# Nine of sixteen products by C on GpSimd instead of eight, in a four-layer selective scan

## The reference

```
dA = exp(d_t[:, :, None] * A)
h = dA * h + (d_t * u_t)[:, :, None] * b_t[:, None, :]
y = einsum('bdn,bn->bd', h, c_t)
```

## Time and profile before

| what | value |
|---|---|
| runs | 2176.87, 2178.3, 2180.0 us |
| median | 2178.3 us |
| the profiled execution's own time | 2175.6 us |
| its span, first to last instruction | 2173.8 us |
| mean granted TensorE clock | 0.942 |
| busy: PE, DVE, ACT, POOL | 1875.8, 1943.6, 1682.6, 1460.3 us |
| stretch of the steps in steady state | about 150 to 1640 us |
| stretch of the experts | about 1732 to 2174 us |

### The profile page before, as it was taken

How to read it: one execution, slowest core, us unless ns; L and a number is a source line. 1 busy time by engine, 2 the same in 40 slices (tenths; PEclk the granted TensorE clock), 3 DMA queues, 4 the chain that set the end, 5 groups by cost and what they waited for, 6 DMA issues and landing times.

```text
span 2173.8 us, 34586 instructions
## 1 busy us (share of the span) xinstructions
PE 1875.8 (86%) x10784; PEld 1179.1 (54%) x10784; DVE 1943.6 (89%) x1824; ACT 1682.6 (77%) x3050; POOL 1460.3 (67%) x1365
## 2 busy tenths in 40 slices
PE   4588888888888888888888888888887599999998
PEld 1344444444444444444454444444444289998998
DVE  3699999999999999999999999999999877776775
ACT  3799999998999999999999898999998233333343
POOL 1588888888888888888888888888889400000000
PEclk8799999999999999999999999999999799999999
DMA  7233232323232323233333323232324100000000
GB/s 235 79 77 84 71 77 61 77 61 77 61 77 62 81 65 80 69 79 77 79 80 80 77 61 77 61 77 61 77 62 119 35 1 11 11 11 10 10 6 11
DMA packets 73289, 139.45 MB, mean 64 GB/s; under 512 B 13072, under 2 KB 31120, under 8 KB 68624
## 3 DMA queue, kind: packets, MB, share of 16 engines
q1 hardware_dynamic: 66832, 120.32, 22.9%
q10 hardware_dynamic: 6400, 18.42, 3.7%
HBM read 63.85 MB, written 7.74 MB: 33 GB/s over the span
## 4 chain that ended last, share of the span: by engine, by line
ACT 29%; POOL 26%; PE 25%; issue 12%; DVE 5%; SPq 1%; DMA 1%; ACTq 1%; POOLq 0%; DVEq 0%
POOL scan L466 12%; ACT decay L545 11%; POOL scan L460 11%; PE y_ps L1216 11%; PE dbu_ps L1192 8%; ACT scan L623 7%; DVE scan L800 3%; POOL scan L457 2%; ACT sp_e L582 2%; ACT delta L583 2%; ACT sp_l L592 2%; PE dbu_ps L1016 2%; ACT sp_e L587 1%; SPq L351 1%; ACT du_t L608 1%
## 5 line engine op out<-in xcount | busy, mean ns | idle before, releaser
L800 DVE TENSOR_TENSOR_SCAN scan<-decay,dbu_ps 128x1024 f32<-128x1024 f32 x512 | 1154.8, 2274 | 47.2 <-PE dbu_ps L1016 40.3
L1016 PE MATMUL dbu_ps<-ident,scan 128*128 128x128 f32 x4096 | 570.4, 286 | 236.4 <-DVE scan L800 198.8
L466 POOL TENSOR_TENSOR scan<-scan,c_rep 128x1024 f32<-128x1024 f32 x256 | 676.3, 2642 | 140.8 <-DVE scan L800 75.8
L1016 PEld LDWEIGHTS dbu_ps<-ident,scan 128*128 128x128 f32 x4096 | 479.8, 146 | 516.6 <-DVE scan L800 266.6
L545 ACT ACTIVATE decay<-d_rep,a_cur 128x510 f32<-128x510 f32 x1024 | 668.1, 709 | 72.0 <-DMA d_rep<-delta 29.6
L460 POOL TENSOR_SCALAR scan<-du_t,b_t 128x256 f32<-128x256 f32 x896 | 592.7, 677 | 0.0
L623 ACT ACTIVATE scan<-du_t,b_t 128x256 f32<-128x256 f32 x1024 | 445.6, 494 | 1.2
L809 DVE TENSOR_TENSOR scan<-scan,c_rep 128x1024 f32<-128x1024 f32 x256 | 330.8, 1292 | 0.0
L738 ACT ACTIVATE decay<-dbu_ps 128x512 f32<-128x512 f32 x256 | 148.5, 598 | 207.0 <-PE dbu_ps L1192 195.6
L1001 PE MATMUL y_ps<-scan,sel 128*32 128x512 f32 x2048 | 301.8, 664 | 5.7 <-POOL scan L466 5.7
L1029 PE MATMUL pre_ps<-xn,w_pre 128*128 128x512 f32 x512 | 248.4, 608 | 5.6 <-DVE w_pre L789 4.8
(11 more groups left out here) (105 smaller groups left out, 1784.5 us busy)
## 6 DMA issues: line engine op xcount, KB each, us to landing
d_rep<-delta SPq DMA_DIRECT2D x512, 128.0 KB, 3.1
c_rep<-c_rows SPq DMA_DIRECT2D x32, 1024.0 KB
w_pre<-prepared_weights ACTq DMA_DIRECT2D x15, 866.0 KB, 13.8
prepared_weights<-scan SPq DMA_DIRECT2D x3, 1122.0 KB, 26.9
scan<-in_conv_w SPq DMA_DIRECT2D x4, 512.0 KB, 4.9
w_out<-prepared_weights SPq DMA_DIRECT2D x16, 128.0 KB, 13.3
sp_e<-in_x_rows SPq DMA_DIRECT2D x8, 256.0 KB, 3.4
d_rep<-in_w ACTq DMA_DIRECT2D x2, 1024.0 KB, 7.3
```

The source lines that it names most:

```text
L466: nc.gpsimd.tensor_tensor(ring[slot % RING], ring[slot % RING], c_rep[par][:, slot // PRS, :].unsqueeze(1).broadcast_to([128, 2, TG]), ALU ...
L800: nc.vector.tensor_tensor_scan(ring[slot % RING].rearrange("p u t -> p (u t)"), decay[slot % DEC].rearrange("p u a t -> p (u a t)"), dbu_p ...
L1016: last = nc.tensor.transpose(dbu_ps[slot % 2][:, u, 128 * j:128 * j + 128], dbu_t[m % 2][:, j, b, :, :].rearrange("p q c -> p (q c)"), ide ...
```

## The change

The slots whose product GpSimd makes are listed in `C_POOL`: the odd ones and slot 8. VectorE makes the seven others. GpSimd makes the product of slot 8 in its slot 9, behind that slot's two outer products and ahead of the wait for `delta`; VectorE no longer makes it between scans 9 and 10. All thresholds that count the products (on TensorE, ScalarE and SP) are counted from the two lists.

```diff
--- before.py
+++ after.py
@@ -28,6 +28,8 @@
 M = NS // Q
 NBC = RANK + 2 * NS
 PRS = UNITS // 2
+C_POOL = [c for c in range(M * PRS) if c % 2 or c == M * PRS // 2]
+C_DVE = [c for c in range(M * PRS) if c not in C_POOL]
 SLOTS = M * PRS
 RING = 8
 DEC = 4
@@ -387,8 +389,8 @@
                     replicate(s + 1, nxt)
                 if is_last(s):
                     sp.wait_ge(skip_done, STEPS)
-                    sp.wait_ge(hc_dve, SLOTS // 2 * (STEPS - 1))
-                    sp.wait_ge(hc_pool, SLOTS // 2 * (STEPS - 1))
+                    sp.wait_ge(hc_dve, len(C_DVE) * (STEPS - 1))
+                    sp.wait_ge(hc_pool, len(C_POOL) * (STEPS - 1))
                     for e in range(EXPERTS):
                         sp.dma_start(w2_sb[e], w2[e, :, :].rearrange("(c p) d -> p c d", p=128))\
                             .then_inc(w2_loaded[e // half], 16)
@@ -481,7 +483,7 @@
                         outer(s + 1, nxt, 0, POOL_FIRST[slot % PRS], POOL_FIRST[slot % PRS + 1])
                     if slot == 0 and has(s, -1):
                         times_c(s - 1, i if par else i - 1, nxt, SLOTS - 1)
-                    elif slot % 2 == 0 and slot and has(s, 0):
+                    elif slot - 1 in C_POOL and has(s, 0):
                         times_c(s, i, par, slot - 1)
                     if slot == 7 and has(s, 2):
                         normalise(s + 2)
@@ -569,8 +571,8 @@
                 nc.scalar.activation(dbc[:, :], pre_ps[0][0:NBC, :], ACT.Copy).then_inc(dbc_ready, 1)
                 act.wait_ge(dbc_ready, s + 1)
 
-                wait(act, hc_dve, SLOTS // 2 * (s - 1))
-                wait(act, hc_pool, SLOTS // 2 * (s - 1))
+                wait(act, hc_dve, len(C_DVE) * (s - 1))
+                wait(act, hc_pool, len(C_POOL) * (s - 1))
                 act.dma_start(c_dram[par, :, :], dbc[RANK + NS:NBC, :]).then_inc(c_stored, 16)
 
             def softplus_parts(s):
@@ -818,7 +820,7 @@
                 for slot in range(SLOTS):
                     if has(s, 0):
                         scan(s, slot)
-                        if slot % 2:
+                        if slot - 1 in C_DVE:
                             times_c(s, i, par, slot - 1)
                     if has(s, -1):
                         if slot == 2:
@@ -994,8 +996,9 @@
                     .then_inc(ms_ready, 1)
 
             def quad(s, m, k):
-                pe.wait_ge(hc_dve, SLOTS // 2 * s + 2 * m + k + 1)
-                pe.wait_ge(hc_pool, SLOTS // 2 * s + 2 * m + k + 1)
+                end = PRS * m + 2 * k + 2
+                pe.wait_ge(hc_dve, len(C_DVE) * s + sum(c < end for c in C_DVE))
+                pe.wait_ge(hc_pool, len(C_POOL) * s + sum(c < end for c in C_POOL))
                 for j in range(Q):
                     slot = PRS * m + 2 * k + j // 2
                     last = nc.tensor.matmul(y_ps[k][CH * j:CH * j + CH, :], sel[:, :],
```

## The result

| kernel | median us | runs | ratio to before, 95% interval | span of the profiled execution |
|---|---|---|---|---|
| before | 2176.9 | 5 | | 2173.8 |
| nine on GpSimd, slot 8 in its slot 9 | 2221.9 | 5 | 1.0206 (1.0192 to 1.022) | 2219.3 |

The change costs 45 us, 2.1%.

The account below looks back on a forecast made before the run. It took a loop through ScalarE, GpSimd and TensorE as the bound, without VectorE's relief. Late `delta` adds 0.7 an even and 0.95 an odd window, with transfers and window 30 +27 us: 2205 us, range 2176 to 2228.

Parts of the forecast that it names:

- The bound: VectorE, though busiest, doesn't set the window; removing its product, 1.3 us a step, by itself buys nothing.
- the loop: ScalarE to `copy_dut`, GpSimd's products, TensorE from slot 0 to `project_z`, ScalarE to the next softplus: 51.43 or 51.18 us.
- The counted loop: From TensorE's transposes of slot 0 to the next window's first softplus instruction: 28.86 us.
- The hold: GpSimd's new product gets in between softplus instructions L835 and L839 and holds L839 up: `delta` 2.03 us late.
- The first rival: VectorE keeps the ports from L835 to L839, `delta` is on time: 2178 to 2205 us, 15%.
- TensorE's passage: From the transposes of slot 11, at half clock, 3.49 us to the start of `turn_du`, which ends at t=12.9.
- The third rival: Late `d_rep` transfers or TensorE's half clock after longer rest put 2.03 us or more into 31 windows: 2241 to 2253, 12%.
- my range: 2176 to 2228 us, meant to hold 8 in 10, widened to take in the rival where the product isn't let in.
- unknown rests: Allowance of 0.2 to 0.6 us a window around the forecast, giving 2190 to 2225 us.
- The transfers: ScalarE's wait for `d_rep` at the next slot 0: a tie, but 1.2 us more in each of two windows.
- the sum: 15 even windows x 0.7, 14 odd x 0.95 and 2 x 1.2: 26.2 us; with window 30, +27.
- The collision that falls away: In odd windows VectorE's product of slot 10 no longer shuts out GpSimd's of slot 11, 2.92 instead of 2.37 us.

Follow-up runs that it names:

- e1: The changed kernel, with GpSimd making the product of slot 8 behind `du`: 2181.1 us, 1.0017 of the kernel before.
- v2: The kernel before, with GpSimd's first outer products one slot earlier and nine products on GpSimd, that of slot 8 behind `du`: 2163.9 us, 0.9936.
- v1: The kernel before, with GpSimd's first outer products of the next step one slot earlier, ahead of the product of slot 11: 2162.7 us, 0.9935.
- e6: The changed kernel, with GpSimd's product of slot 8 cut into two instructions of 512 elements at the same place: 2176.6 us, 1.0001.

## Why the prediction was right, and where its size was off

**The bound.** That VectorE isn't in the loop at 89% busy was right: with 1.3 us less of its work, e1 and v2 gain nothing. That the loop goes through GpSimd's outer products is shown by v1, which shortens just that link. The counted loop (28.86 from the transposes of slot 0 to the next softplus) held in the changed kernel too: 892.16 - 863.28 = 28.88.

**The hold.** Forecast: L839 ends at t=5.94. Measured: 841.55 + 3.26 - 838.88 = 5.93. Scan 9 forecast over at 8.05, transposes of slot 11 at 8.19; measured 847.07 - 838.88 = 8.19. The first rival (the product isn't let in) is refuted by the 3.26. In window 0 of the changed kernel it was the second softplus instruction that was held instead (3.26), and in window 30 neither; both are single windows.

**The step that failed: TensorE's passage.** "From their start to the start of `turn_du` it is 828.47 - 824.98 = 3.49", and then 1.2 for `turn_du`: 4.69 in all, at the end of which the clock was back. That is the passage of window 14, and I carried it over to every window. In the changed kernel it is 5.73 in the even windows: `turn_du` starts at t=11.95 (forecast 11.7) and ends at 13.9 (forecast 12.9), `copy_dut` at 853.44 - 838.88 = 14.56 (forecast 13.4). In window 15 `turn_du` takes 1.13 and `copy_dut` ends at 904.92 + 1.09 - 892.16 = 13.85; in most odd windows it is 14.1, as the first softplus instruction is longer there by 0.3. So the transposes of slot 0 come at 24.40 and 23.56, where I had 23.3: windows 14 and 15 grew by 1.85 and 1.25, not by 0.7 and 0.95, and the mean over the 30 windows is 1.45.

It doesn't take the longer rest for that. The trace of the kernel before has the slow passage too, after the same 4.55 us of rest as in window 14. This is its window 2:

```profile
208.73 1.97 PE L1016 MATMUL dbu_ps<-ident,scan 128*128 128x128 f32 x8 [4.55 <-DVE scan L800]
210.63 1.93 PE L1001 MATMUL y_ps<-scan,sel 128*32 128x512 f32 x8
212.49 1.97 PE L1094 MATMUL pre_ps<-ident,sp_l 128*128 128x128 f32 x8
```

From 208.73 to 214.46 it is 5.73. Of the 30 windows of the kernel before, only windows 11 to 18 are at 4.66 to 4.73; the other 22 are at 5.08 to 5.74. The mean is 5.26, and in the changed kernel 5.29, after rests of 6.58 and more. I had read one window of the favourable kind. Before the change this didn't matter: in window 2 `turn_du` ends at t=11.9 and `copy_dut` still ends at 12.87. With scan 9 2.03 later the slow kind ends at 13.9, on the path. The third rival named TensorE's half clock, but put it down to the longer rest and priced it as all or nothing. That the measured time lies within my range, 6 us below its upper end, is owed in part to the range's width, which stood there for unknown rests and not for this.

**The transfers.** I charged 2.4 us for two windows with late transfers and expected ScalarE's wait for `d_rep` to grow to 1.7. Neither came: no period of the changed kernel is above 53.3, and among its waits of 400 to 1400 us there is none for `d_rep`. In window 14 of the kernel before, the decays of the next slot 0 waited for the transfers until 835.70 - 818.82 = 16.9, and 2.03 later would be 18.9. In the changed kernel they start at 857.10 - 838.88 = 18.2, without a wait. The rows are of before and after:

```profile
835.70 1.33 ACT L545 ACTIVATE decay<-d_rep,a_cur 128x510 f32<-128x510 f32 x2 [0.27 <-DMA d_rep<-delta]
...
857.10 1.31 ACT L547 ACTIVATE decay<-d_rep,a_cur 128x510 f32<-128x510 f32 x2
```

So the transfers that slot 0 needs were less than 2.03 later. They landed sooner after their issue: 2.6 to 3.2 us in this window, against 3.1 to 8.0 in window 14 of the kernel before. Why is not shown. One smaller slip: the sum has 14 odd windows where 15 lie ahead of window 30, which is 1 us.

**The collision that falls away.** Right: GpSimd's product of slot 11 takes 2.37 or 2.38 in every window. It is small against the rest.

## What to carry to other kernels

Before work is moved to GpSimd, look at what VectorE does at that moment, not at GpSimd's idle time: a wait in front of a GpSimd instruction that ends with a VectorE result is a place where VectorE may be running instructions of the kind that were held here, and a long GpSimd instruction there can hold VectorE up for nearly its own length (2.03 us by one of 2.37). If it must stand there, cut it: four pieces cost nothing that can be measured here (1.0008, 0.9997 to 1.0019) where one cost 2%. And take the busiest engine for the bound only after the chain and the waits say so: taking work off the engine that was 89% busy gained nothing, while a new order on the one that was 67% busy (v1) gained 0.65%. And take a duration that follows a rest of TensorE from many windows of the trace, not from one.

## What the runs showed of the hardware that I had not expected

TensorE's clock came back at different times after rests of the same length: in e6, after 5.50 us, `turn_du` took 1.10 us in one window and 1.97 in the next, with the same instructions ahead of it. In the changed kernel, after 6.58 us, it took 1.97 in the even window and 1.13 in the odd one. In the kernel before, the passage behind the rest shrinks step by step from window to window after rests of 4.55 to 4.66 us (5.53 us in window 4, 5.42 in window 6, 5.27 in window 8, 5.11 in window 10, 4.69 in window 12) and is back at 5.44 in window 20. A duration behind a rest is therefore not one number; a sum that uses it needs its spread.
